# Token sums put together on VectorE, statistics and keys sooner, and a second scatter table, in a one-core attention and mixture-of-experts layer

## The reference, cut to what matters

```
# attention: no softmax; one vector A per sequence
Xn = layernorm(xn, gamma, beta);  Q, K, V = split(Xn @ W_in + b_in)
K, V = rotary(K), rotary(V)                  # first 128 columns
A = 0.5 * sum_tokens(K/|K| * V/|V|) + 0.5    # [2, 256]
att = (A[:, None, :] * Q) @ W_out + b_out + xn
# feed-forward: 16 experts, top 4 per token, capacity 128 rows for an expert
scores = softmax(xn @ gate_w.T); top 4, normalized
eout[e] = (silu(xg @ w_gate[e]) * (xg @ w_up[e])) @ w_down[e] * weight
y[token] += eout                              # scatter-add over 16 experts
shared = silu(xn @ sw_gate) * (xn @ sw_up) @ sw_down
```

## Time and profile before

| | |
|---|---|
| median of 3 runs | 166.44 us (165.03 to 167.22) |
| the profiled execution | 163.03 us, of which the span from first to last instruction is 161.2 us |
| busy: TensorE / VectorE / GpSimd / ScalarE | 93% / 67% / 58% / 47% |
| DMA | 28.53 MB, mean 177 GB/s |
| mean granted TensorE clock | 0.997 |

### The profile page before, as it was taken

The page is one execution under the profiler, slowest core; times in us unless marked ns, Lnnn a source line. Parts: engine busy times, 40 slices in busy tenths (PEclk is TensorE's granted clock), DMA queues, the critical chain, the costliest instruction groups (busy, mean ns, idle before and its releaser), DMA issues. The chain is left out here.

```text
span 161.2 us, 3124 instructions
## 1 busy us (share of the span) xinstructions
PE 150.7 (93%) x1005; PEld 133.4 (83%) x1005; DVE 108.4 (67%) x322; ACT 75.3 (47%) x226; POOL 94.0 (58%) x123
## 2 busy tenths in 40 slices
PE   7989859999999999999999999999899999999970
PEld 5567649999886889988889989987799897889970
DVE  0898999678867465988488878743884151484980
ACT  3053546685468976667475645371342163410000
POOL 8678789571337928837855995647533333303470
PEclk9999999999999999999999999999999999999998
DMA  4999989982003558575568755759562211329577
GB/s 147 324 365 354 457 334 354 342 292 34 2 8 104 178 192 176 167 144 112 166 198 187 170 157 107 177 152 226 82 157 33 31 16 22 33 36 341 180 266 255
DMA packets 25523, 28.53 MB, mean 177 GB/s; under 512 B 4130, under 2 KB 24579, under 8 KB 25476
## 3 DMA queue, kind: packets, MB, share of 16 engines
q1 hardware_dynamic: 21058, 22.90, 43.9%
q0 software_dynamic: 3072, 4.33, 16.3%
q10 hardware_dynamic: 1378, 1.12, 2.2%
HBM read 21.64 MB, written 8.79 MB: 189 GB/s over the span
## 5 line engine op out<-in xcount | busy, mean ns | idle before, releaser
L435 POOL DMA_INDIRECT ysum<-eo,idx x16 | 29.6, 1848 | 32.2 <-DMA ysum<-eo,idx 18.9
L247 PE MATMUL bank<-wkvr_s,xt_all 128*128 128x256 f32 (+1 forms) x96 | 29.3, 305 | 2.3 <-DVE xt_all L697 0.9
L249 PE MATMUL bank<-wkvr_s,xt_all 128*128 128x256 f32 (+1 forms) x96 | 27.2, 283 | 0.0
L248 PE MATMUL bank<-wkvr_s,xt_all 128*128 128x256 f32 (+1 forms) x96 | 27.1, 282 | 0.0
L427 POOL DMA_INDIRECT xg<-rows,idx x16 | 19.6, 1222 | 7.7 <-issue 4.3
L1176 PE MATMUL bank<-xgt,wgu 128*128 128x128 f32 (+1 forms) x192 | 24.0, 275 | 0.0
L1176 PEld LDWEIGHTS bank<-xgt,wgu 128*128 128x128 f32 (+1 forms) x192 | 22.4, 187 | 0.1
L247 PEld LDWEIGHTS bank<-wkvr_s,xt_all 128*128 128x128 f32 x96 | 18.1, 188 | 4.2 <-DVE xt_all L697 1.9
L247 PE MATMUL bank<-xt_all,sw_s 128*128 128x512 f32 (+1 forms) x48 | 20.8, 434 | 0.0
L248 PE MATMUL bank<-xt_all,sw_s 128*128 128x512 f32 (+1 forms) x48 | 18.9, 394 | 0.0
L249 PE MATMUL bank<-xt_all,sw_s 128*128 128x512 f32 (+1 forms) x48 | 18.9, 394 | 0.0
(11 more groups left out here) (167 smaller groups left out, 345.4 us busy)
## 6 DMA issues: line engine op xcount, KB each, us to landing
wgu<-in_w_gu SPq DMA_DIRECT2D x16, 368.0 KB, 3.4
rows<-xn_all SPq DMA_DIRECT2D x4, 512.0 KB, 7.6
wdn<-in_w_dn SPq DMA_DIRECT2D x16, 128.0 KB, 3.6
x_all<-ysum SPq DMA_DIRECT2D x4, 512.0 KB, 5.6
x_all<-in_x SPq DMA_DIRECT2D x3, 512.0 KB, 7.1
trg<-in_trig SPq DMA_DIRECT2D x1, 1024.0 KB, 6.1
out<-xn_all ACTq DMA_DIRECT2D x4, 256.0 KB, 3.3
out<-xn_all SPq DMA_DIRECT2D x4, 256.0 KB, 3.1
```

The lines of the kernel that those rows point to most:

```text
L247: nc.tensor.matmul(dst, lt_hi, r_hi, start=start, stop=False)
L248: nc.tensor.matmul(dst, lt_hi, r_lo, start=False, stop=False)
L249: return nc.tensor.matmul(dst, lt_lo, r_hi, start=False, stop=stop)
L435: nc.gpsimd.indirect_dma_start(out=ysum, out_offset=bass.IndirectOffsetOnAxis(ap=idx[:, e:e + 1], axis=0), in_=eo[:, e % G, :], in_offset= ...
```

## The change

- **Token sums.** After the last accumulation of a sequence VectorE adds the rotary halves itself (`together`: four small instructions). `reduce_tokens` has two matmuls instead of four, and `combine`, `sums` and the constant tables of `combine` (2 x 128 columns of `consts`) go. The waits on `acol_done` move: TensorE now waits before the transpose that follows.
- **Statistics and keys.** Tiles 2, 3 and 8 to 11 (`BY_ACT`) get mean and sum of squares on ScalarE (`means`, `squares`: four activations with accumulation for a pair of tiles). `KEY_STEPS` has keys 0 to 7 at t = 4 to 11; the key weights are folded at t = 1 and split at t = 2 instead of 4 and 5. Warm-up is 4 matmuls, TensorE waits for only the first of GpSimd's three small instructions before its first fold, and VectorE's order in the first 10 us is rewritten.
- **Second table.** Experts 12 to 15 scatter to `ysum[1]`, zeroed by one DMA of 2176 rows of 1 KB, placed on SP after the weights of expert 3 and ahead of the saves of `wd`. `ysum[0]` is read back once scatter 11 has landed, into `x_all`; `ysum[1]` after scatter 15, into `vr_all`. Each group is added twice: from `ysum[0]`, groups 0 and 1 on GpSimd at e = 14 and 15 (between scatters 13, 14 and 15), groups 2 and 3 on VectorE after the loop; from `ysum[1]`, groups 0 and 3 on VectorE, 2 and 1 on GpSimd, as before but later in VectorE's list.

```diff
-WARM_UP = 5
+WARM_UP = 4
+SECOND = 12
+BY_ACT = (1, 4)
-KEY_STEPS = ((), (), (), (), (), (), (), (0,), (1,), (2,), (3,), (4,), (5,), (6,), (), (7,))
+KEY_STEPS = ((), (), (), (), (0,), (1,), (2,), (3,), (4,), (5,), (6,), (7,), (), (), (), ())
...
             load_expert(3)
+            sp.dma_start(ysum_v[1], zero[:, 0:D].unsqueeze(1).to_broadcast([P, TILES + 1, D])).then_inc(pads_saved, 16)
             sp.wait_ge(wd_pool, 1)
...
-            sp.wait_ge(scat_done, 16 * E)
-            for g in (2, 3, 0, 1):
-                sp.dma_start(yin[:, g * G:(g + 1) * G, :], ysum_v[:, g * G:(g + 1) * G, :]).then_inc(y_in[g], 16)
+            for k, last, order in ((0, SECOND - 1, (0, 1, 2, 3)), (1, E - 1, (2, 3, 0, 1))):
+                sp.wait_ge(scat_done[k], 16 * scattered(last)[1])
+                for g in order:
+                    sp.dma_start(yin[k][:, g * G:(g + 1) * G, 0:D], ysum_v[k][:, g * G:(g + 1) * G, :]).then_inc(y_in[k][g], 16)
...
             def scatter(e):
+                k, n = scattered(e)
                 pool.wait_ge(eo_done, e + 1)
-                if e:
-                    pool.wait_ge(scat_done, 16 * e)
+                if n > 1:
+                    pool.wait_ge(scat_done[k], 16 * (n - 1))
...
                 if e in WEIGHTS:
                     weights(WEIGHTS[e])
+
+                if e >= E - 2:
+                    pool.wait_ge(kept, 4)
+                    for t in range(G * (e - E + 2), G * (e - E + 3)):
+                        add_y(0, t)
             scatter(E - 1)
...
+            def means(t):
+
+                act.wait_ge(x_in[load_of(t)], 16)
+                for j in range(2):
+                    nc.scalar.activation(junk[:, j, :], x_all[:, t + j, :], ACT.Copy, scale=-1.0 / D, accum_out=nm[:, t + j:t + j + 1]).then_inc(mean_done, 1)
...
+            def together(b):
+
+
+                half = acc[:, b, :].rearrange("p (q a n) -> p q a n", q=4, a=2)
+                dve.wait_ge(acc_done, TILES_B * (b + 1))
+                nc.vector.tensor_tensor(acc[:, b, 2 * P:3 * P], acc[:, b, 2 * P:3 * P], acc[:, b, 3 * P:4 * P], ALU.add).then_inc(pre_done, 1)
...
             def reduce_tokens(b, e):
 
-                pe.wait_ge(acc_done, TILES_B * (b + 1))
+                pe.wait_ge(pre_done, 4 * b + 4)
                 pe.wait_ge(xgt_done, e + 2)
-                for q in range(4):
-                    last = nc.tensor.matmul(bank[4][:, q:q + 1], acc[:, b, q * P:(q + 1) * P], one_col[:, :], start=True, stop=True)
-                last.then_inc(red_done, 1)
+                nc.tensor.matmul(bank[4][:, 0:1], pre[:, b, :], one_col[:, :], start=True, stop=True)
+                nc.tensor.matmul(bank[4][:, 1:2], acc[:, b, P:2 * P], one_col[:, :], start=True, stop=True).then_inc(red_done, 1)
```

More of the change, by code:

```diff
@@ L229, in layer @@
         rows_v = rows.rearrange("(t p) d -> p t d", p=P)
-        ysum_v = ysum.rearrange("(t p) d -> p t d", p=P)
+        ysum_v = [y.rearrange("(t p) d -> p t d", p=P) for y in ysum]
         w_v = w_in.rearrange("(c p) n -> p c n", p=P)
@@ L285, in _ @@
             save_xn(0)
-            sp.dma_start(ysum[0:TOKENS, :], x_rows).then_inc(ysum_set, 16)
+            sp.dma_start(ysum[0][0:TOKENS, :], x_rows).then_inc(ysum_set, 16)
             sp.wait_ge(zero_set, 1)
             sp.dma_start(rows[TOKENS:TOKENS + CAP, :], zero).then_inc(pads_saved, 16)
-            sp.dma_start(ysum[TOKENS:TOKENS + CAP, :], zero[:, 0:D]).then_inc(pads_saved, 16)
+            sp.dma_start(ysum[0][TOKENS:TOKENS + CAP, :], zero[:, 0:D]).then_inc(pads_saved, 16)
             save_xn(1)
@@ L480, in _, with squares @@
             nc.scalar.activation(one_junk[:, :], one_col[:, :], ACT.Exp).then_inc(table_set, 1)
+            def means(t):
+                act.wait_ge(x_in[load_of(t)], 16)
+                for j in range(2):
+                    nc.scalar.activation(junk[:, j, :], x_all[:, t + j, :], ACT.Copy, scale=-1.0 / D, accum_out=nm[:, t + j:t + j + 1]).then_inc(mean_done, 1)
+            def squares(t):
+                n = squares_of(next(k for k, (a, b) in enumerate(ROOTS) if a <= t < b)) - ROOTS[next(k for k, (a, b) in enumerate(ROOTS) if a <= t < b)][1] + t
+                act.wait_ge(mean_done, n + 2)
+                if n:
+                    act.wait_ge(sq_done, n)
+                for j in range(2):
+                    nc.scalar.activation(junk[:, 2 + j, :], x_all[:, t + j, :], ACT.Square, bias=nm[:, t + j:t + j + 1], accum_out=mv[:, t + j, 1:2]).then_inc(sq_done, 1)
             def weights_hi(k, cs_, n, after):
@@ L538, in _ @@
                     hi_pair(t // 2 + 1)
-                if t == 5:
+                if t in (0, 2):
+                    means(8 + t)
+                if t in (1, 3):
+                    squares(7 + t)
+                if t == 2:
                     weights_hi(2, slice(0, DC), slice(VR, VRK), 5)
@@ L957, in _ @@
                 if e in SUMS:
-                    sums(SUMS[e])
+                    columns(SUMS[e])
                 for i in KEYS[e]:
@@ L964, in _ @@
                     rotate(i)
+                if e + 1 in SUMS:
+                    together(SUMS[e + 1])
+            dve.wait_ge(kept, 6)
+            add_y(0, 2)
             shared_mid(10, unit_bank(E - 1))
             shared_lo(10)
+            add_y(0, 3)
             shared_mid(11, unit_bank(E))
```

178 lines of the change are left out of this document (95 added, 83 removed).

## The result

The kernel before takes 165.74 us in the comparison (median, 163.15 to 167.22), the changed one 172.31 us (170.23 to 174.17): ratio 1.046, interval 1.023 to 1.069. The forecast was 164.2 us in a range of 161.2 to 166.9, so the change is slower where "no change" was forecast, and outside the range. A ratio leaves out the executions that lie over 1.5% above the fastest of their kernel, a median takes all of them; executions of one kernel lie 3 to 5% apart, so small differences are read from the traces.

What follows compares the result with a forecast made beforehand. TensorE, busy 150.7 of 161.2 us, and the scatters were two chains ending together. Front 1.5 plus sums 1.0 less 0.3 ends VectorE 2.2 us sooner, GpSimd 2.3; 2.2 off gives 164.2 us, range 161.2 to 166.9.

Steps and rivals of the forecast that it cites:

- One warm-up less is 4.63 / 5 = 0.93 us: At TensorE's start: one warm-up matmul fewer makes the start 0.7 us sooner, between 0 and 0.93.
- lie in a time in which it waits for shared units: nothing: In the tail: VectorE's early adds of groups 2 and 3 from the first table cost nothing.
- I take 0.8 us (0 to 3): Scatters 12 and 13 beside the 2 MB readback of the first table: 0.8 us lost, between 0 and 3.
- the scatter chain holds the end: Rival, at the end: scatter 12 or 13 takes 3 us more, add rounds 0.7 each; about 167 us; chance 0.10.
- scatter steps over 6 us at 12 and 13: Sign that the forecast is wrong: steps of the scatter chain over 6 us at experts 12 and 13.
- VectorE or GpSimd the difference, 0.7 us a round: New adds on VectorE and GpSimd shut each other out of SBUF, costing one of them 0.7 us a round.
- 3.3 - 0.4 - 2.1 = 0.8 us sooner: Front: tile 12 ends 0.8 us sooner, from TensorE's waits of 3.3, less 0.4 for ScalarE and 2.1 for keys.
- I count 0.7 us for that: Front, from tile 12 to the last mask: VectorE waits less in its list, 0.7 us gained (0 to 1.4).
- Zero fill at nothing: Zeroing the second table ahead of the gather costs nothing; the fill takes 6.4 us, until about 41.8.
- The slower rival: On SP's queue ahead of the `wd` saves: the fill at half rate delays everything behind 3.9 us; 168.1 us; chance 0.08.
- Token sums, 1.0 us of TensorE's end: Two matmuls instead of four and no `combine`: 1.0 us a sequence, the first spent waiting, the second counted.
- begun as soon as before: Tail: outputs of 2 MB take 6.4 us at 330 GB/s and start no later, leaving 4.3 us after VectorE's end.

Runs made afterwards that it cites:

- with six: Six warm-up matmuls in place of four in the changed kernel; 167.16 us, ratio 1.021 against the kernel before.
- with five: Five warm-up matmuls in place of four in the changed kernel; 166.44 us, ratio 1.017 against the kernel before.
- the table kernel: Only the second table, put on the kernel before; 166.92 us, ratio 1.023.
- With the clock and the adds mended: Changed kernel with five warm-ups and VectorE's two adds of the first table behind its mixes of tiles 1 to 7; 164.44 us, ratio 0.998 against the kernel before.
- the front alone and five warm-ups: Only ScalarE's statistics, the sooner keys and the reordered start, put on the kernel before, with its five warm-ups kept; 165.83 us against 164.7.
- the changed kernel, repeated: The changed kernel, four warm-ups, measured again on one chip with the six-warm-up kernel; 169.85 us, ratio 1.022 against the kernel before.

## Why the prediction was wrong

- **"One warm-up less is 4.63 / 5 = 0.93 us", "I take 0.7 us of start, between 0 and 0.93".** This is the step that failed first. A warm-up was priced as work removed, from the earlier trace rows, and nothing was asked of the work behind it. The next matmuls doubled, the gather came 3.8 us later instead of 1.5 sooner. The bounds, 0 and 0.93, had no loss in them. What it costs at the end is open, between nothing and 3%.
- **VectorE's early adds "lie in a time in which it waits for shared units: nothing".** The second failure, and the one that every comparison bears out. Two adds of 1.2 us would fit that time; the wait ahead of the first and the slowing of the second beside GpSimd don't. The landing was priced for GpSimd's chain only; on VectorE everything behind the wait stood for 1.1 us with six, 2.3 with five and 5.1 in the changed kernel (where the scatters, and so the readback, were later still than the start made them), and TensorE paid 2.7 to 3.4 us and then 3 to 5 us at a lower clock. Moving the two adds takes 1.9% off at five and at least as much at four.
- **"I take 0.8 us (0 to 3)" for scatters beside the readback.** The mechanism was named, the term mis-sized: 4.1 us. The rival "the scatter chain holds the end" had 3 us and was the nearer one, at a chance of 0.10; the case against it, that sharing would slow a scatter "by its own few hundred ns", was ten times too small. The sign "scatter steps over 6 us at 12 and 13" came for 13 (8.2 us in the changed kernel), not for 12 (4.9). "Scatter 12 within 0.4 us behind 11" held: 0.30.
- **"VectorE or GpSimd the difference, 0.7 us a round", by the rule of shutting out** (Trainium skill, SBUF — State Buffer, section Who interferes with whom). The trace agrees, in a larger size. Changed kernel with five, GpSimd's and VectorE's timelines:

```profile
137.54 4.16 POOL L479 TENSOR_TENSOR xn_all<-xn_all,x_all 128x256 f32<-128x256 f32 x4
```

```profile
134.07 1.23 DVE L1008 TENSOR_TENSOR xn_all<-xn_all,x_all 128x1024 f32<-128x1024 f32 x1 [2.29 <-DMA x_all<-ysum_a]
...
137.33 3.89 DVE L1008 TENSOR_TENSOR xn_all<-xn_all,x_all 128x1024 f32<-128x1024 f32 x1
```

  The same add takes 1.23 us alone and 3.89 beside GpSimd's four, which take 4.16 for 2.6 to 3.1. That is 2.7 us on VectorE ahead of `shared_mid(11)`, which the prediction had left out of its sum. (In the changed kernel's profiled execution the two didn't meet: 1.22 and 3.12.)
- **Front, "3.3 - 0.4 - 2.1 = 0.8 us sooner" and "I count 0.7 us for that".** The sum of 1.5 us holds only one of its two terms of 0.7, the start or the list; with both it is 2.2. It is wrong at five and six warm-ups too: gathers between 46.50 and 48.76 for 46.63, 46.50 to 46.90 in four of seven. TensorE's waits move rather than go; left out are the waits that the new order makes and, as far as one trace tells, the eighth key ahead of the last tile.
- **Zero fill at nothing: right**, 0 to 0.4 us. It ran at 379 to 391 GB/s from 39 to 44 us. It wasn't over by 42: issued at 36.45, it landed 10.6 us later, in the table kernel 10.4 us behind 33.05. The changed kernel's DMA issues (KB each, us from issue to landing) show that the first save behind it did wait, 6.3 us for 3.5 before, but the last one, ahead of the gather, took 1.8 us as before: the slack was enough. The slower rival, a gather held by the fill, falls; the two faults above were in no rival. By the rule of ring order (Trainium skill, DMA: Bandwidth & Descriptors, section Queues, rings and completion order) a save behind the fill should wait for it, and the trace agrees: issued at 39.68, the save landed about 46.0, when the fill's traffic ended (302 GB/s from 44 to 45 us, 96 from 45 to 46).

```profile
ysum_b<-acc SPq DMA_DIRECT2D x1, 2176.0 KB, 10.6
...
rows<-wd SPq DMA_DIRECT2D x1, 64.0 KB, 6.3
```

- **Token sums, 1.0 us of TensorE's end: near.** With the clock and the adds mended TensorE ends 1.7 us sooner with a gather as before, but that is the whole change's. Alone they are worth nothing in time (ratio 0.998) and 0.6 us of TensorE's end in one trace (155.48 for 156.05). There TensorE waits 1.6 us for `together` at the first sequence, where the prediction took nothing (0.2 us in the changed kernel), and the readback, at 145.09, is no sooner, so the other chain holds the end, as the first paragraph of the prediction says of a gain in one.
- **Tail.** Outputs "begun as soon as before" was near: 153.49 to 153.68 in the kernels with five and the adds late, for 153.90. But it bounds the whole change: with both losses mended the profiled span is 160.8 for 161.2, not 159.0.

The profiled spans go from 170.8 us as changed to 166.3 with the fifth warm-up and 160.8 with VectorE's adds late too, for 161.2 before. So both faults mended leave no loss. The steps, 4.5 and 5.5 us, are no prices: they compare single executions, the gather is 3.1 us of the first, and the medians differ by 2.0 us in the second (166.44 and 164.44). The third fault, the scatters beside the readback, eats what the second table gains, so that nothing is gained once the two are mended.

## What to carry to other kernels

Before removing warm-up work, ask what the engine's next instructions cost at its lower level, not what the warm-up costs: here 0.9 us removed made the first gather 2.3 to 4.2 us late, though how much of that reached the end varied from nothing to 3%. When work is moved into an engine's idle time, price the wait ahead of it, and what runs beside it, against the instruction that is queued behind it: two adds of 1.2 us that nothing needed yet held VectorE for 5 to 7 us and cost TensorE 3 us and then its clock. A transfer moved into a quiet stretch can slow the small transfers that already live there, here one of 3.9 us by 4.1; pacing it by their landings gave 2.1 us of that back, which counts only where their chain is the one that ends last.

## What the runs showed that I had not expected

The column of granted clock says 1.00 over 5 to 20 us in the kernels with four warm-ups, while the same matmuls there take twice as long:

```profile
5.00:10.00 5.00, 5.00 (x13) 2.83 (x13) 2.62 (x10) 2.32 (x9) 2.23 (x5) 1.00 1.08 349
```

(the changed kernel, repeated; x13 in 5 us). At the end of the kernel the column does fall, to 0.50 to 0.59, with the same doubling. So at the start the lower level is to be read from durations. The column can fall there too, once TensorE has been at full speed: with the front alone and five warm-ups, a wait of 1.84 us before the first product was followed by matmuls of double length from 12.1 to 15.7 us, and the column says so:

```profile
13.00:14.00 1.00, 1.00 (x4) 0.88 (x4) 0.00 (x0) 0.69 (x3) 0.83 (x3) 0.50 1.01 380
```

The whole change with five waits 1.58 us at that place and stays at 1.00; what tells the two apart no run shows.
